# Reordering the gate block between two attention layers, and moving GpSimd's long operations, in a fused four-layer cross-attention kernel

## What is computed

```
x = _L0_xattn_ref(x, ctx, ctx, mask, ...)   # 16 heads of 64: softmax(Q K^T / 8), masked by query rows, times V, @ W_O.T + b_O + x
# _L1_xattn_ref: the gate block
text_proj = jnp.einsum('blh,oh->blo', text_feat, Wt) + bt
vision_proj = jnp.einsum('bkh,oh->bko', vision_pooled, Wv) + bv      # vision_pooled: mean of the context over its rows
agreement = jnp.sum(text_proj * vision_proj, axis=-1, keepdims=True)
for _ in range(NUM_ITERATIONS):                                      # 3
    routing_weights = jax.nn.softmax(coupling, axis=1)
    weighted_vision = routing_weights * vision_proj
    gate = jax.nn.sigmoid(text_proj @ Wg_t.T + weighted_vision @ Wg_v.T + bg)
    fused = text_feat + gate * weighted_vision
    coupling = coupling + agreement
out = (fused - mu) / jnp.sqrt(var + LN_EPS) * gamma + beta
# _L2_xattn_ref: 16 heads of 16, Q from x, K and V from the context, ReLU on all three, causal,
#   keys whose K row sums to zero masked, ReLU(out @ Wo + bo) + x, normalised with ddof=1
# _L3_xattn_ref: self-attention in a band of 64 with a slope per head, cross-attention to the context
#   without a mask, then a GELU MLP of width 1024; each with residual and layer norm
```

## Time and profile before

| | |
|---|---|
| median of 3 runs | 1923.41 us |
| the profiled execution | 1930.14 us, its span 1928.2 us |
| TensorE (matmuls) busy | 1645.5 us, 85% |
| VectorE busy | 941.0 us, 49% |
| ScalarE busy | 736.9 us, 38% |
| GpSimd busy | 254.0 us, 13% |
| TensorE's clock over the span | 0.913 of full |

### The profile page before, as it was taken

The page is one execution under the profiler, slowest core; times in us unless marked ns, Lnnn a source line. Parts: engine busy times, 40 slices in busy tenths (PEclk is TensorE's granted clock), DMA queues, the critical chain, the costliest instruction groups (busy, mean ns, idle before and its releaser), DMA issues.

```text
span 1928.2 us, 27173 instructions
## 1 busy us (share of the span) xinstructions
PE 1645.5 (85%) x9552; PEld 846.1 (44%) x9592; DVE 941.0 (49%) x2240; ACT 736.9 (38%) x1281; POOL 254.0 (13%) x116
## 2 busy tenths in 40 slices
PE   5999886879999988778999898877899988869786
PEld 2236555434424555532532454553263255546234
DVE  2653654462455465456156446445525635635551
ACT  1642333264263242426236325142624621614352
POOL 1012110200101311110010211120011031112001
PEclk9998998879999899887999989988899998989788
DMA  8001103402100211240210030223021003031300
GB/s 308 1 6 34 34 15 53 99 1 104 45 1 6 37 31 30 38 99 1 104 45 1 6 53 15 46 55 66 26 80 45 1 13 60 2 62 41 53 23 11
DMA packets 44869, 84.17 MB, mean 44 GB/s; under 512 B 10417, under 2 KB 28593, under 8 KB 44465
## 3 DMA queue, kind: packets, MB, share of 16 engines
q1 hardware_dynamic: 44288, 78.42, 17.3%
q10 hardware_dynamic: 432, 3.83, 0.5%
HBM read 42.37 MB, written 2.10 MB: 23 GB/s over the span
## 4 chain that ended last, share of the span: by engine, by line
issue 35%; PE 32%; DVE 18%; ACT 6%; POOL 4%; SPq 3%; DMA 1%; DVEq 0%; ACTq 0%; POOLq 0%
DVE nmax L894 6%; PE ring L1034 5%; PE obank L1245 4%; PE ring L1013 4%; DVE region_d L778 3%; PE ring L1226 3%; PE ring L1025 2%; PE ring L1286 2%; ACT region_e L595 2%; SPq L370 2%; PE ring L1044 2%; POOL q_all L518 2%; ACT region_e L671 1%; PE obank L1006 1%; ACT q_all L663 1%
## 5 line engine op out<-in xcount | busy, mean ns | idle before, releaser
L894 DVE TENSOR_REDUCE nmax<-ring 128x2 f32<-128x1024 f32 (+4 forms) x384 | 309.2, 852 | 255.6 <-PE ring L1195 165.9
L671 ACT ACTIVATE region_e<-ring 128x1024 f32<-128x1024 f32 (+4 forms) x384 | 267.9, 734 | 216.3 <-PE ring L1195 96.2
L778 DVE CUSTOM_DVE_ANT_0 region_d<-ring,maskb 128x512 f32<-128x512 f32 x256 | 165.8, 686 | 118.0 <-issue 117.8
L595 ACT ACTIVATE region_e<-region_d,nmin 128x512 f32<-128x512 f32 x256 | 182.5, 714 | 92.1 <-DVE nmin L778 86.1
L663 ACT ACTIVATE q_all<-ring 2x1024 fp32r<-2x1024 bf16 x96 | 97.6, 1016 | 213.4 <-PE ring L1256 212.3
L1006 PE MATMUL obank<-cbf 128*128 128x512 bf16 x632 | 165.2, 402 | 4.9 <-issue 3.3
L1195 PE MATMUL ring<-cbf 64*128 64x128 bf16 (+1 forms) x2048 | 166.8, 248 | 0.0
L1072 PE MATMUL obank<-region_e,vs 128*64 128x512 f32 x512 | 139.9, 630 | 15.1 <-DVE vs L764 15.1
L1226 PE MATMUL ring<-q_all,k_tiles_a 64*128 64x512 f32 (+4 forms) x384 | 88.3, 463 | 71.2 <-ACT region_e L671 52.5
L1062 PE MATMUL ring<-region_q 64*128 64x512 f32 x512 | 141.3, 636 | 5.4 <-ACT region_q L584 5.4
L1209 PE MATMUL ring<-k_tiles_a,q_all 64*128 64x512 f32 (+4 forms) x384 | 89.7, 477 | 55.6 <-DMA q_all<-q_parts 45.2
(11 more groups left out here) (169 smaller groups left out, 2278.5 us busy)
## 6 DMA issues: line engine op xcount, KB each, us to landing
q_all<-q_parts SPq DMA_DIRECT2D x288, 64.0 KB, 2.3
k_tiles_a<-k_parts SPq DMA_DIRECT2D x144, 64.0 KB, 2.3
k_tiles_b<-k_parts SPq DMA_DIRECT2D x144, 64.0 KB, 2.3
region_b<-in_w_f SPq DMA_DIRECT2D x8, 1024.0 KB, 4.9
wvo<-in_wv SPq DMA_DIRECT2D x4, 1024.0 KB, 9.0
wqk<-in_wq SPq DMA_DIRECT2D x4, 1024.0 KB, 10.9
wqk<-in_wk SPq DMA_DIRECT2D x4, 1024.0 KB, 12.9
wvo<-in_wo SPq DMA_DIRECT2D x4, 1024.0 KB, 5.6
```

What stands on the lines that cost most here:

```text
L595: ins = act.activation(e0[:, n % E0, h, :], sm0[:, n % 2, h, :], ACT.Exp, bias=nmin0[:, n, h:h + 1], scale=-1.0, accum_out=sum0[:, n, h:h ...
L671: act.activation(e16[:, n % 4, 2 * u:2 * u + 2, 0:nq], slot((a, "B", g, kt, u))[:, :, 0:nq], ACT.Exp)\
L778: ins = dve.tensor_tensor_reduce(out=sm0[:, n % 2, h, :], in0=slot(("S0", p, kt))[:, h, :], in1=maskb[:, :], scale=-1.0, scalar=3.0e38, op ...
L894: dve.tensor_reduce(nmax[:, qt, 2 * u:2 * u + 2], slot(name)[:, :, 0:nk], AX.X, ALU.max, negate=True)\
```

## The change

Nothing is computed otherwise; instructions change places and one buffer moves.

- **Tail of layer 0.** `vp` is placed ahead of the last pair's value products, `K2` between the third and the last of them, `vpT` behind them. `uv` and `ksum` go between the two halves of `O0`.
- **Gate block.** The halves of `V2` go to either side of `tp`; `rcol` goes between the two halves of `gate`; `VC` comes ahead of `X1` instead of after `meanO`; `keep_warm` ahead of `X1` has 12 products instead of 18. On VectorE the multiply and add behind the sigmoid go in two halves, and the masks of v (`mask_v`, 8 operations) are spread around the norm.
- **GpSimd.** `reset_tiles` begins when layer 0's heads are all copied out (`out_drained`) instead of at the last score product, and `k_tiles_a` no longer waits for `O0`; `residual(0)` and `put_ones` wait for the first pass A of the CAUSAL attention.
- **k_parts** moves from unit 1 to unit 2 of `e16`, and ScalarE's wait for the k copies from the first exponential to the one at kt = 2.

The diff, cut to its core (TensorE's new functions `out_project0`, `values2` and `gate` hold the products of before, a half at a time, and are left out):

```
-    jobs += [("O0", j) for j in range(2)]
-    jobs += [("vp",), ("vpT",), ("X", 0), ("K2",), ("uv",), ("tp",), ("ksum",), ("agree",)] + [("gate", j) for j in range(2)]
-    jobs += [("rcol",)] + [("V2", j) for j in range(2)] + [("cnt",), ("X", 1), ("Q2",), ("meanV",), ("meanO",)]
-    jobs += [("VC", j) for j in range(2)]
+    jobs += [("vp",), ("K2",), ("vpT",), ("O0", 0), ("uv",), ("ksum",), ("O0", 1)]
+    jobs += [("X", 0), ("V2", 0), ("tp",), ("V2", 1), ("agree",), ("gate", 0), ("rcol",), ("gate", 1), ("cnt",)]
+    jobs += [("VC", j) for j in range(2)] + [("X", 1), ("Q2",), ("meanV",), ("meanO",)]
...
-        k_parts = overlay("k_parts", at_e + 4 * 2048, [P, 2, DT, S])
+        k_parts = overlay("k_parts", at_e + 2 * 4 * 2048, [P, 2, DT, S])
...
                 def reset_tiles():
 
-                    pool.wait_ge(*filled_by(("S0", PAIRS - 1, NT - 1), b))
+                    pool.wait_ge(out_drained, b * OUT_ITER + PAIRS)
                     zeros = zero[:, 0:1].unsqueeze(2).broadcast_to([P, 4, S])
...
-                    pool.wait_ge(pv_done, b * PV_ITER + UNITS0)
+                    rows_of_k = cb("keyrows", S).unsqueeze(1).broadcast_to([P, 4, S])
+                    pool.tensor_tensor(k_tiles_a[:, :, :], rows_of_k, zeros, ALU.add).then_inc(tiles_reset, 1)
                     for j in range(2):
...
                         pool.wait_ge(*filled_by(("O0", j), b))
-                    rows_of_k = cb("keyrows", S).unsqueeze(1).broadcast_to([P, 4, S])
-                    for tiles in (k_tiles_a, k_tiles_b):
-                        pool.tensor_tensor(tiles[:, :, :], rows_of_k, zeros, ALU.add).then_inc(tiles_reset, 1)
+                    pool.tensor_tensor(k_tiles_b[:, :, :], rows_of_k, zeros, ALU.add).then_inc(tiles_reset, 1)
...
+                pool.wait_ge(*filled_by((CAUSAL, "A", 0, 0, 0), b))
                 residual(0, "ga1", "be1")
 
-                pool.wait_ge(*filled_by(("VC", 0), b))
                 put_ones(v_of[FULL])
...
-                act.wait_ge(*filled_by(("vpT",), b))
-                act.activation(wide[:, :, :], slot(("vpT",))[:, 0, 0:D].rearrange("p (t n) -> p t n", t=DT), ACT.Copy)\
-                    .then_inc(*ends_drain(("vpT",)))
...
+                act.wait_ge(pv_done, b * PV_ITER + UNITS0 - 2)
+                drain_k(("K2",), CAUSAL, 0, ACT.Relu)
+                act.wait_ge(*filled_by(("vpT",), b))
+                act.activation(wide[:, :, :], slot(("vpT",))[:, 0, 0:D].rearrange("p (t n) -> p t n", t=DT), ACT.Copy)\
+                    .then_inc(*ends_drain(("vpT",)))
                 drain_x(0)
-                drain_k(("K2",), CAUSAL, 0, ACT.Relu)
...
-                                if g == 0 and which == [0, 0, 0]:
+                                if which == [0, 2, 0]:
                                     for k in range(1, GROUPS):
                                         act.wait_ge(k_stacked[k], (b * 3 + a + 1) * 96)
...
+                dve.wait_ge(*filled_by(("vp",), b))
+                dve.tensor_tensor(vp_b[:, :], slot(("vp",))[:, 0, 0:D], row("bv1").squeeze(1), ALU.add).then_inc(*ends_drain(("vp",)))
                 scale_v(UNITS0 - 1)
                 drain_heads0(PAIRS - 2)
                 drain_heads0(PAIRS - 1)
```

VectorE, as it stands after the change between layer 0 and `Q2`:

```
+                dve.wait_ge(resid0_ready, b + 1)
+                drain_o0(0)
+                dve.wait_ge(*filled_by(("uv",), b))
+                dve.tensor_copy(u_b[:, :], slot(("uv",))[:, 0, 0:D]).then_inc(*ends_drain(("uv",)))
+                dve.wait_ge(*filled_by(("ksum",), b))
+                dve.tensor_scalar(km[:, :], slot(("ksum",))[:, 0, 0:NT], 0.0, None, ALU.is_gt).then_inc(*ends_drain(("ksum",)))
+                drain_o0(1)
+                drain_v("V2", "bv2", lambda t: v2[:, t, :].rearrange("p (h c) -> p h c", h=H))
+
+                dve.wait_ge(*filled_by(("agree",), b))
+                link(dve.tensor_reduce(one_sum[0:1, 0:1], slot(("agree",))[0:1, 0, :], AX.X, ALU.max))
...
+                mask_v(0)
+                dve.wait_ge(*filled_by(("rcol",), b))
...
+                mask_v(1)
+                for j in range(2):
+                    part = slice(2 * j, 2 * j + 2)
+                    dve.wait_ge(gate_ready, b * 2 + j + 1)
+                    for t in (2 * j, 2 * j + 1):
+                        ins = dve.scalar_tensor_tensor(out=nat_y[:, t, :], in0=vp_b[:, :], scalar=rcol[:, t:t + 1], in1=nat_n[:, t, :],
+                                                       op0=ALU.mult, op1=ALU.mult)
+                    link(ins)
+                    link(dve.tensor_tensor(nat_y[:, part, :], nat_y[:, part, :], nat_x[:, part, :], ALU.add))
                 dve.wait_ge(*filled_by(("cnt",), b))
                 dve.tensor_scalar(degen[:, :], slot(("cnt",))[:, 0, 0:NT], 0.5, None, ALU.is_lt).then_inc(*ends_drain(("cnt",)))
+                norm(0)
+                for t in (2, 3):
+                    mask_v(t)
+                drain_v("VC", "cbv", lambda t: v_of[FULL][:, t, :, 0:DH])
```

TensorE:

```
-                        keep_warm(18)
+                        keep_warm(12 if n == 1 else 18)
...
+                for kt in range(NT - 1):
+                    values0(PAIRS - 1, kt)
                 project(("K2",), w_sq["k2"], ctx_t, range(DT))
+                values0(PAIRS - 1, NT - 1)
+                dst = start(("vpT",))
...
+                out_project0(0)
                 dst = start(("uv",))
...
+                out_project0(1)
+                for j in range(2):
+                    pe.wait_ge(*drained_by(("O0", j), b))
+                turn(0, nat_x)
+                values2(0)
+                pe.wait_ge(*drained_by(("X", 0), b))
+                project(("tp",), w_l1["t"], act_t, range(DT))
+                values2(1)
                 dst = start(("agree",))
...
+                gate(0)
 
                 dst = start(("rcol",))
...
+                gate(1)
...
+                pe.wait_ge(k_loaded["lc"], 64)
+                project_nat("VC", w_sq["cv"], ctx_t)
                 turn(1, nat_n)
...
-                pe.wait_ge(vmask_ready, b + 1)
+                pe.wait_ge(vmask_ready, (b + 1) * NT)
...
-                pe.wait_ge(k_loaded["lc"], 64)
-                project_nat("VC", w_sq["cv"], ctx_t)
```

More of the change, by code:

```diff
@@ L791, in _ @@
                 dve.wait_ge(resid0_ready, b + 1)
-                for j in range(2):
-                    dve.wait_ge(*filled_by(("O0", j), b))
-                    dve.scalar_tensor_tensor(out=nat_x[:, 2 * j:2 * j + 2, :], in0=slot(("O0", j))[:, :, 0:D], scalar=nanfix[:, 3:4],
-                                             in1=x_nat[:, 2 * j:2 * j + 2, :], op0=ALU.add, op1=ALU.add)\
-                        .then_inc(*ends_drain(("O0", j)))
-                dve.wait_ge(*filled_by(("vp",), b))
-                dve.tensor_tensor(vp_b[:, :], slot(("vp",))[:, 0, 0:D], row("bv1").squeeze(1), ALU.add).then_inc(*ends_drain(("vp",)))
                 def drain_v(name, bias, dst):
```

122 lines of the change are left out of this document (57 added, 65 removed).

## The result

The changed kernel takes 1878.38 us (median of 4 runs, 1873.01 to 1880.01); the kernel before, run beside it, 1924.62 us (1919.04 to 1926.26). The ratio is 0.9757 (95% interval 0.9735 to 0.978): 46 us faster, where 68 were forecast. It lies 1.4 us above the range of 1839 to 1877; one of the four executions, the profiled one, lies inside it.

What follows compares the result with a forecast made beforehand. Hand-overs between engines, a chain of waits, were taken to bound the kernel. Per pass 7.6 + 5.4 - 0.8 - 0.5 + 5.3 = 17.0, 68 over four: profiled 1930.14 becomes 1862, about 1856 as median; range 1839 to 1877 us.

Steps and rivals of the forecast that it cites:

- Gate: X0 to batch statistics: reordered work starts the statistics at 650.2, not 659.57; gain 9.4 us.
- up to X1: Statistics to X1, limited by TensorE's clock: X1 at 655.9, gaining 7.6 us a pass, with 4.1 and 10.1 as ends.
- X1 to pass A: From X1 to the first pass A: 13.5 us instead of 18.9, gain 5.4 (4.5 to 5.6).
- the row at 0.66: Profile row with clock 0.66 from 648.2 to 663.4; by it TensorE is through at 656.5 before X1; 655.9 was taken.
- Tail: Layer 0's end: K2 refills GpSimd's lock, so little is gained; X0 starts at 628.0 against 628.32, gain 0.3 us.
- GpSimd: Behind pass A, moved operations hold VectorE's cast and subtraction of the maxima: 0.8 us lost, bounds 0 and 1.8.
- the prediction's sentence on the page: Skill page's rule: two-SBUF-input VectorE work contends with GpSimd reading SBUF, the second blocks fully; so the subtraction is held.
- Gain 5.3, bounds 4 and 6.5: BANDED attention: exponentials of kt 0 and 1 run inside ScalarE's stall for the k copies; 5.3 us a pass.
- In CAUSAL and FULL the k copies are landed in any case: 0: CAUSAL and FULL attentions: moving k_parts and ScalarE's wait gains 0, since nothing waits for the k copies there.
- BANDED gives nothing: Rival: BANDED's wait only moves, a group 0 product hanging on a later copy; 11.7 a pass, 1876 us, chance 0.08.
- The clock eats more: Rival: clock low through VC, the warm products and the first passes A; 12 us a pass, 1875 us, chance 0.15.
- signs of being wrong: Half clock behind cnt over 7 us, cast of maxima waiting over 2 us for GpSimd, or a new ring-slot drain wait.

Runs made afterwards that it cites:

- residual_late_in_before: The kernel before, with only residual(0) and put_ones made to wait for the CAUSAL attention's first pass A: 1924.3 us, ratio 0.9993.
- vc_late: The changed kernel with the two VC jobs behind meanO again, on TensorE and VectorE: 1877.12 us, ratio 0.9736.
- resets_early: The changed kernel with reset_tiles beginning at the last score product again and k_tiles_a behind pv_done: 1880.63 us, ratio 0.9784.
- warm26_in_stall: The changed kernel with 26 warm TensorE products in BANDED's stall, ahead of group 0's pass B of kt = 3: 1862.88 us, ratio 0.9686.
- kparts_warm: The kernel before with k_parts in unit 2, ScalarE's wait at kt = 2 and 26 warm products in BANDED's stall: 1897.42 us, ratio 0.9873.
- warm_causal: The changed kernel with 9 warm products ahead of narrow passes B in groups 1 to 3 of the CAUSAL attention: 1871.94 us, ratio 0.9712.
- combined_w26: The changed kernel with 4 warm products ahead of X1, residual(0) behind first pass B, 9 warm products in CAUSAL, 26 in BANDED's stall: 1851.25 us.
- residual_early: The changed kernel with residual(0) as soon as the norm is ready and put_ones at VC, as before: 1880.78 us, ratio 0.9778.

## Why the prediction was wrong

- **Gate, up to X1, X1 to pass A.** Right, each within 0.2 us a pass. The weight of the row at 0.66 in the `X1` term was right on the mean (5.2 us in three passes, 6.8 in pass 3, forecast 5.7), and the copies bound pass A, as worked out. But the masks and `VC` are worth nothing one at a time: with the masks' hold gone alone, `X1` to pass A is 16.6 to 18.5 us and the time stays (residual_late_in_before), with `VC` back alone it is 15.6 to 16.9, made up by an earlier `X1` (vc_late). Only with both out of the way did the q copies become the bound.
- **Tail.** Right that it gains little; 0.3 us a pass was -0.15: `O0` starts 0.1 us sooner instead of 0.5. resets_early shows why GpSimd's move is worth so little: with `K2` as cover its hold costs 0.26 us.
- **GpSimd.** The place was right, the operation not: the cast was held (0.86), the subtraction behind it not (0.23). It started after GpSimd's end, so these rows do not test what the prediction's sentence on the page says of it. Hold and cold start cost 0.7 us a pass instead of 1.3.
- **BANDED. "Gain 5.3, bounds 4 and 6.5".** This step failed. 3.3 us a pass were measured. The exponentials did move into the stall, and the wait fell from 41.3 us to 21.9 over four passes. But the term took the time of group 1 from a trace in which the low stretch ended as group 1 began (both at 791.6); with group 1 5 us closer to the stall it lies on group 1. Shown by warm26_in_stall and kparts_warm, which have 4.9 without it.
- **"In CAUSAL and FULL the k copies are landed in any case: 0".** This failed too. The copies are no loss there, but they are the only reason given for 0, and the clock inside an attention that is not edited has no term. The CAUSAL one cost 7.2 us in three passes, by the clock. Shown by its rows (42.3 us at 1.00, 44.6 at 0.92, the same work) and by warm_causal, at 1.00 in all passes.
- **The profile against the median.** The forecast scaled by one execution of the kernel before. Executions of one kernel differed by 0.1% (combined_w26) to 0.9% (residual_early, 1873.24 to 1889.66). That low stretches fall otherwise in each of them is likely, as they do from pass to pass, but only profiled executions show where they fall; for the others it is left open.
- **Rivals.** "BANDED gives nothing", 1876, is the nearest in time and false, since it gives 3.3 us a pass. "The clock eats more", 1875, has the right kind of cause, but its places were wrong: not `VC` (but for pass 3), `X1` or the first passes A, but an attention 30 us later and the far side of a stall. Of the signs of being wrong that were named, none looks at either place. Why a given start of the CAUSAL attention brings none, one or two low stretches is not settled by these runs, only that its work alone does not decide it.

## What to carry to other kernels

When an edit removes waits, TensorE's clock prices more of the time: go through all that follows, also what the diff does not touch, at both levels of the clock, and look at it pass by pass. In the stall tried here half a filling gave nothing and a whole one 15 us, while 14 products more ahead of another wait lost 7: cost each by a run. To learn whether a slow stretch hangs on its work or on its moment, delay it by a us or two and add nothing else, and read the clock ahead of it too.
